# Attention with split-precision matmuls: values products of 512 columns, half of the long ones turned into x's place

## The reference

```python
# x: [1024, 512]; 32 query heads, 8 key/value heads, 32 latent heads, head size 128
q  = rope(x @ w_q);  k = rope(x @ w_k);  v = x @ w_v
lq = x @ w_lq;       lk = rope(lq @ w_lk);  lv = x @ w_lv
attn = causal_attn(q, repeat(k, 4), repeat(v, 4))     # softmax(q k^T / sqrt(128)) v
lat  = causal_attn(q, lk, lv)
x = layernorm(x + attn @ w_o + lat @ w_lo)
# top-1 routed low-rank FFN
logits = x @ route_w.T;  route_weight = one_hot(argmax) * max
out = ((route_weight[..., None] * (x @ A)) @ Bw)
x = layernorm(x + out)
```

## Time and profile before

| what | value |
|---|---|
| median of 3 runs | 2001.11 us (2000.52 to 2001.81) |
| the profiled execution | 2000.62 us |
| its span, first to last instruction | 1998.5 us |
| PE busy | 1974.5 us (99%), 12640 matmuls |
| DVE, POOL, ACT busy | 1352.9, 1127.4, 1064.4 us |
| mean granted TensorE clock | 0.999 |

### The profile page before, as it was taken

The page is one execution under the profiler, slowest core; times in us unless marked ns, Lnnn a source line. Parts: engine busy times, 40 slices in busy tenths (PEclk is TensorE's granted clock), DMA queues, the critical chain, the costliest instruction groups (busy, mean ns, idle before and its releaser), DMA issues.

```text
span 1998.5 us, 33651 instructions
## 1 busy us (share of the span) xinstructions
PE 1974.5 (99%) x12640; PEld 1804.9 (90%) x12640; DVE 1352.9 (68%) x3370; ACT 1064.4 (53%) x2463; POOL 1127.4 (56%) x904
## 2 busy tenths in 40 slices
PE   8999999999999999999999999999999999999997
PEld 7989989899898989989899898998989989898995
DVE  7758668585675757757577684766757577575766
ACT  3736628365372744727357373563726547274564
POOL 6637566375664647646475564656646565564750
PEclk9999999999999999999999999999999999999999
DMA  5010010101000010000100001000010100100001
GB/s 179 12 35 1 22 35 12 35 1 44 12 22 25 1 56 1 22 25 1 56 1 22 24 5 52 1 22 25 22 35 1 42 5 22 35 12 22 1 12 43
DMA packets 19296, 50.14 MB, mean 25 GB/s; under 512 B 5824, under 2 KB 7872, under 8 KB 19008
## 3 DMA queue, kind: packets, MB, share of 16 engines
q1 hardware_dynamic: 18992, 45.90, 6.9%
q10 hardware_dynamic: 144, 2.10, 0.2%
HBM read 45.89 MB, written 2.10 MB: 24 GB/s over the span
## 4 chain that ended last, share of the span: by engine, by line
PE 88%; POOL 5%; DVE 4%; ACT 2%; issue 1%; DMA 0%; ACTq 0%; SPq 0%; DVEq 0%
PE ps L388 25%; PE ps L390 25%; PE ps L389 25%; PE ps L474 13%; POOL probs L827 3%; POOL ql_lo L831 2%; DVE probs L883 1%; DVE probs L882 1%; DVE probs L884 1%; ACT probs L660 1%; DVE val_lo L848 0%; DVE probs L908 0%; ACT ql_hi L631 0%; ACT acc L727 0%; PE ps L587 0%
## 5 line engine op out<-in xcount | busy, mean ns | idle before, releaser
L836 POOL TENSOR_TENSOR probs<-probs,inv_sum 128x640 f32<-128x640 f32 (+7 forms) x512 | 583.4, 1151 | 343.7 <-DVE inv_sum L915 342.7
L908 DVE CUSTOM_DVE_ANT_0 probs<-ps,mask 128x640 f32<-128x640 f32 (+7 forms) x512 | 384.6, 754 | 167.1 <-PE ps L390 120.3
L848 DVE TENSOR_TENSOR pt_lo<-ps,pt_hi 128x512 fp32r<-128x512 f32 (+3 forms) x768 | 399.2, 548 | 74.9 <-ACT pt_hi L631 73.1
L631 ACT ACTIVATE pt_hi<-ps 128x512 fp32r<-128x512 f32 (+3 forms) x768 | 347.0, 487 | 163.6 <-PE ps L474 160.3
L660 ACT ACTIVATE probs<-probs,neg_max 128x640 f32<-128x640 f32 (+7 forms) x512 | 396.9, 775 | 61.0 <-DVE neg_max L908 49.9
L388 PE MATMUL ps<-pt_hi,val_hi 128*128 128x256 f32 x1216 | 353.8, 291 | 0.0
L389 PE MATMUL ps<-pt_lo,val_hi 128*128 128x256 f32 x1216 | 342.6, 282 | 0.0
L390 PE MATMUL ps<-pt_hi,val_lo 128*128 128x256 f32 x1216 | 342.3, 282 | 0.0
L474 PE MATMUL ps<-ident,probs 128*128 128x128 f32 x2304 | 335.0, 273 | 0.0
L827 POOL TENSOR_TENSOR probs<-probs 128x512 f32<-128x512 f32 x144 | 186.5, 1295 | 210.7 <-DVE probs L884 210.7
L631 ACT ACTIVATE ql_hi<-probs 128x512 fp32r<-128x512 f32 x128 | 80.9, 632 | 415.3 <-POOL probs L827 415.3
(11 more groups left out here) (101 smaller groups left out, 4099.6 us busy)
## 6 DMA issues: line engine op xcount, KB each, us to landing
raw<-wo SPq DMA_DIRECT2D x32, 512.0 KB, 3.3
raw<-wq SPq DMA_DIRECT2D x16, 512.0 KB, 3.2
raw<-wlv SPq DMA_DIRECT2D x16, 512.0 KB, 3.7
raw<-wkv SPq DMA_DIRECT2D x8, 512.0 KB, 3.4
acc<-xT SPq DMA_DIRECT2D x4, 512.0 KB, 5.5
wlk_raw<-wlk SPq DMA_DIRECT2D x16, 128.0 KB, 3.1
acc<-x ACTq DMA_DIRECT2D x1, 2048.0 KB, 10.3
out<-acc SPq DMA_DIRECT2D x8, 256.0 KB, 2.0
```

Of the source, the lines that this page charges most:

```text
L631: return nc.scalar.activation(dst, src, ACT.Copy)
L836: nc.gpsimd.tensor_tensor(b, b, inv_sum[:, k % 8:k % 8 + 1].to_broadcast([P, b.shape[-1]]), ALU.mult).then_inc(q["normed"], 1)
L848: return nc.vector.tensor_tensor(dst, src, h, ALU.subtract)
L908: nc.vector.tensor_tensor_reduce(out=probs_of(n).rearrange("p (b n) -> p b n", b=b), in0=scores_of(n), in1=mask[:, S - w:S].rearrange("p ( ...
```

## The change

- Values products cover four query tiles, 512 columns, and there are 8 per pair (`CHUNKS = TILES // 4`). Even products take the short tiles of a latent head or of the plain heads, odd ones the long tiles. Block j of a product starts at the first column that needs it (`first_column`). `PV_BEFORE` and `PV_AFTER` place them: slots 13, 16, 21, 24, 29, 31, 36, 36.
- Odd products hold 8 blocks x 512 columns of turned probabilities. Products 3 and 7 have them in parts 0 and 1 of `pt_hi`, `pt_lo`; products 1 and 5 in `x_hi`, `x_lo` (`turned_probs`). x is therefore stored once in device memory (`x_kept`) and read back in every pair but the last (`bring_x_back`: four DMAs on ACT's queue behind the high part of product 5). PE waits for it (`x_back`) ahead of the two units of query head 0.
- The order of units changes; three `v` units instead of one are put off into the attention slots.
- The first two units of pair 1 (both `lk`) are made in the outputs stage of pair 0 (`AHEAD`).
- The order of output steps and tiles, the slots of output weights and the slots of the high and low parts of products (`O_SLOT`) change; `HI_LAG` is 2; one output is added in slot 37.

```diff
@@
-CHUNKS = TILES // 2
+STEP_ORDER = ((1, 0), (0, 0), (1, 1), (0, 1))
+CHUNKS = TILES // 4
-O_BANKS = (6, 7)
+O_BANKS = (7, 6, 6, 7)
+LATE_BANKS = (6, 7)
-OUT_HI_SLOT = (16, 24)
-OUT_LO_TILE = (17, 25)
+OUT_HI_SLOT = (20, 27)
+OUT_LO_TILE = (19, 31)
-    [("q", 0, 0), ("q", 0, 1), ("lk", 0, 0), ("v", 0), ("lk", 0, 1), ("v", 1), ("q", 1, 0), ("q", 1, 1), ("lk", 1, 0), ("v", 2), ("lk", 1, 1), ("v", 3), ("k", 0, 0), ("k", 0, 1), ("v", 4), ("v", 5), ("v", 6), ("v", 7)],
-    [("q", 0, 0), ("lk", 0, 0), ("q", 0, 1), ("v", 0), ("lk", 0, 1), ("q", 1, 0), ("v", 1), ("lk", 1, 0), ("q", 1, 1), ("v", 2), ("lk", 1, 1), ("v", 3), ("v", 4), ("v", 5), ("v", 6), ("v", 7)],
+    [("q", 0, 0), ("q", 0, 1), ("lk", 0, 0), ("v", 0), ("lk", 0, 1), ("q", 1, 0), ("v", 4), ("lk", 1, 0), ("q", 1, 1), ("v", 1), ("lk", 1, 1), ("k", 0, 0), ("k", 0, 1), ("v", 5), ("v", 2), ("v", 6), ("v", 3), ("v", 7)],
+    [("lk", 0, 0), ("lk", 0, 1), ("q", 0, 0), ("lk", 1, 0), ("q", 0, 1), ("v", 0), ("lk", 1, 1), ("q", 1, 0), ("v", 4), ("q", 1, 1), ("v", 1), ("v", 5), ("v", 2), ("v", 6), ("v", 3), ("v", 7)],
-LATE = ({6: 17}, {6: 15})
+LATE = ({4: 15, 7: 16, 10: 17}, {3: 13, 7: 14, 9: 15})
-OUT_ORDER = tuple(i for pair in HEADS_AT_ONCE for i in pair)
-HEAD = {34: ((0, 0, 2),), 35: ((1, 0, 2), (2, 0, 2)), 36: ((0, 2, 4), (1, 2, 4))}
+OUT_ORDER = (3, 2, 4, 5, 1, 0, 6, 7)
+HEAD = {32: ((0, 0, 2),), 34: ((1, 0, 2),), 35: ((2, 0, 2), (0, 2, 4)), 36: ((1, 2, 4),)}
+def tiles_of(m):
+    return range(m // 2 * 8 + 1 - m % 2, m // 2 * 8 + 8, 2)
+def column_of(n):
+    a, latent, i = tile_of(n)
+    return P * (i % 4) if latent else 256 * (i % 2) + P * a
+def first_column(m, j):
+    return min(column_of(n) for n in tiles_of(m) if tile_of(n)[2] >= j)
+PV_BEFORE = {13: ((0, 0, 4),), 21: ((2, 0, 4),), 29: ((4, 0, 4),), 36: ((6, 0, 2),)}
+PV_AFTER = {16: ((1, 0, 8),), 24: ((3, 0, 8),), 31: ((5, 0, 6),), 36: ((7, 0, 8),)}
+O_SLOT = {16: (0,), 19: (1,), 22: (2,), 27: (3,), 29: (4,), 34: (5,), 36: (6,), 38: (7,)}
+AHEAD = ({}, {5: (0,), 6: (1,)})
+ADD_SLOT = {37: (0,)}
-HI_LAG = 3
+HI_LAG = 2
@@ def block_kernel
+        kept = nc.dram_tensor("x_kept", [2, 2, P, CT * 512], F32, kind="Internal").ap()
+        def turned_probs(m):
+            if m % 2 == 0:
+                return [w[:, 2, :].rearrange("p (j n) -> p j n", n=512) for w in (pt_hi, pt_lo)]
+            if m % 4 == 1:
+                return [w[:].rearrange("p c (h n) -> p (c h) n", h=2) for w in (x_hi, x_lo)]
+            return [w[:, 0:2].rearrange("p a (j n) -> p (a j) n", n=512) for w in (pt_hi, pt_lo)]
+        def x_half(h):
+            return [w[:, :, 512 * h:512 * h + 512].bitcast(F32) for w in (x_hi, x_lo)]
@@ unit
+                    if kind == "q" and x == 0 and (g, pair) != (0, 0):
+                        pe.wait_ge(x_back[h], 32 * (g * PAIRS + pair))
@@ with_values
                 for j in range(j0, j1):
-                    q0 = P if latent and j == last else 0
-                    at = 256 * (first + j)
-                    mm = three(ps[:, O_BANKS[m % len(O_BANKS)], 256 * (m % 2) + q0:256 * (m % 2) + 256], [w[:, j, :] for w in vals],
-                               [w[:, half, at + q0:at + 256] for w in (pt_hi, pt_lo)], j == 0, j == last)
+                    q0 = first_column(m, j)
+                    mm = three(ps[:, bank, q0:512], [w[:, j, :] for w in vals], [w[:, j, q0:512] for w in turned_probs(m)],
+                               j == 0, j == last)
@@ scalar
+            def bring_x_back():
+                for h in range(2):
+                    for part, dst in enumerate(x_half(h)):
+                        nc.scalar.dma_start(dst, kept[h, part].rearrange("p (c n) -> p c n", c=CT)).then_inc(x_back[h], 16)
@@ scalar, start
             nc.scalar.dma_start(acc[:], x).then_inc(q["res_in"], 16)
+            for h in range(2):
+                for part, src in enumerate(x_half(h)):
+                    nc.scalar.dma_start(kept[h, part].rearrange("p (c n) -> p c n", c=CT), src).then_inc(q["x_saved"], 16)
@@ scalar, slots
-                        if k in O_SLOT:
-                            output_hi(g, pair, O_SLOT[k])
+                        for m in O_SLOT.get(k, ()):
+                            output_hi(g, pair, m)
+                            if m == 5 and (g, pair) != (GROUPS - 1, PAIRS - 1):
+                                bring_x_back()
```

More of the change, by code:

```diff
@@ L145, in bank_of, with values_until @@
 def bank_of(pair, u):
-    return 4 + u % BANKS if u < regular(pair) else O_BANKS[u - regular(pair)]
+    return 4 + u % BANKS if u < regular(pair) else LATE_BANKS[(u - regular(pair)) % 2]
+def values_until(pair, u):
+    return sum(x[0] == "v" for x in UNITS[pair][:u + 1])
 def unit_in_bank(pair, u):
@@ L241, in block_kernel @@
         raw_in = [sem(f"raw_in{i}") for i in range(RAW_SLOTS)]
+        x_back = [sem(f"x_back{h}") for h in range(2)]
         def per_pair(g, pair, n, k):
@@ L476, in turn_probs, with with_values @@
                     mm.then_inc(q["turned"], 1)
[L478 to L482, removed]
+            def with_values(g, pair, m, j0, j1):
+                a, latent, _ = tile_of(max(tiles_of(m)))
+                last = blocks_of_product(m) - 1
+                bank = O_BANKS[m % len(O_BANKS)]
                 if j0 == 0:
-                    pe.wait_ge(q["pt_lo_made"], per_pair(g, pair, T_UNITS, UNITS_BEFORE[n + 1]))
-                    if m == 0:
+                    pe.wait_ge(q["pt_lo_made"], per_pair(g, pair, T_UNITS, UNITS_BEFORE[max(tiles_of(m)) + 1]))
+                    if m < 2:
                         pe.wait_ge(q["val_lo_made"], per_pair(g, pair, ST, ST))
                         pe.wait_ge(q["rope_mul"], rope_base(g, pair, ROPES[pair]))
-                    if m >= len(O_BANKS):
-                        pe.wait_ge(q["o_lo_made"], per_pair(g, pair, CHUNKS, m - len(O_BANKS) + 1))
+                    else:
+                        user = max(x for x in range(m) if O_BANKS[x % len(O_BANKS)] == bank)
+                        pe.wait_ge(q["o_lo_made"], per_pair(g, pair, CHUNKS, user + 1))
                 vals = [w[:, 1 + a if latent else 0] for w in (val_hi, val_lo)]
                 for j in range(j0, j1):
-                    q0 = P if latent and j == last else 0
-                    at = 256 * (first + j)
-                    mm = three(ps[:, O_BANKS[m % len(O_BANKS)], 256 * (m % 2) + q0:256 * (m % 2) + 256], [w[:, j, :] for w in vals],
-                               [w[:, half, at + q0:at + 256] for w in (pt_hi, pt_lo)], j == 0, j == last)
+                    q0 = first_column(m, j)
+                    mm = three(ps[:, bank, q0:512], [w[:, j, :] for w in vals], [w[:, j, q0:512] for w in turned_probs(m)],
+                               j == 0, j == last)
                 if j1 == last + 1:
@@ L508, in outputs @@
                 for step in range(step0, step1):
[L509 to L513, removed]
+                    latent, a = STEP_ORDER[step]
+                    if y == 0 and latent:
+                        pe.wait_ge(q["wo_lo"], SEED + per_pair(g, pair, len(OUT_PARTS), a + 1))
+                        pe.wait_ge(q["o_lo_made"], per_pair(g, pair, CHUNKS, 2 * (a + 1)))
+                    if (latent, a) == (0, 0):
+                        pe.wait_ge(q["o_lo_made"], per_pair(g, pair, CHUNKS, chunk_with(t) + 1))
                     out, weights = output_step(step)
@@ L523, in _ @@
                 for pair in range(PAIRS):
-                    for u in range(regular(pair)):
+                    for u in range(units_ahead(g, pair), regular(pair)):
                         if u == regular(pair) - EARLY_UNIT:
@@ L553, in _ @@
                             outputs(g, pair, y, BEGUN.get(y, 0), STEPS)
+                        for u in begun_behind(g, pair, y):
+                            unit(*next_pair(g, pair), u)
             ra = raw[:, 0, 0:CT * (E + E * R)].rearrange("p (c n) -> p c n", c=CT)
@@ L647, in probs_hi @@
             def probs_hi(g, pair, n):
-                half, first, q0 = part_of_pt(n)
-                dst = pt_hi[:, half, :].rearrange("p (j n) -> p j n", j=ST)
+                q0, dst = column_of(n), turned_probs(chunk_of(n))[0]
+                if (g, pair, n) == (0, 0, 0):
+                    act.wait_ge(q["x_saved"], 64)
                 for x, (b0, b1) in enumerate(blocks_of(n)):
@@ L669, in rope_hi @@
             def rope_hi(g, pair, r):
+                u = ROPE_UNITS[pair][r]
+                if u < units_ahead(g, pair) and UNITS[pair][u][2] == 1:
+                    act.wait_ge(q["out_mm"], SEED + per_pair(g, pair, ST, 0))
                 act.wait_ge(q["rope_add"], rope_base(g, pair, r + 1))
@@ L893, in probs_lo @@
             def probs_lo(g, pair, n):
-                half, first, q0 = part_of_pt(n)
-                h, l = (w[:, half, :].rearrange("p (j n) -> p j n", j=ST) for w in (pt_hi, pt_lo))
+                q0, (h, l) = column_of(n), turned_probs(chunk_of(n))
                 for x, (b0, b1) in enumerate(blocks_of(n)):
```

(14 more changed lines are left out.)

89 lines of the change are left out of this document (43 added, 46 removed).

## The result

The changed kernel takes 2020.99 us (median of 4 runs, 2019.74 to 2022.30) against 2001.46 beside it: ratio 1.0096, 95% interval 1.0078 to 1.0113. It is 1.0% slower where I had forecast 1.4% faster. Both the time and the direction are wrong.

The account below looks back on a forecast made before the run. The prediction took PE to bound the kernel. From 2000.6 us it took 24 (width) and 12 (changes of kind) and added 6 (waits) and 2 (start): 1972.6, rounded to 1973 us, 1.4% faster, range 1959 to 1995.

Parts of the forecast that it names:

- (a): Attention slots without a values product: PE waits for DVE between nothing and 4.8 us a pair; 0.4 taken, 6 us.
- (b): POOL subtracts output weights before scaling tile 20 for slot 24: hidden; if not, about 1 us a pair.
- (c): Reading x back from slot 34 on ACT's queue: landing hidden behind PE's work, issue holding 1.5 us, at no cost.
- fewer changes of kind: Attention slots: fewer values products behind transposes, more scores behind them; saves 0.74 us a pair, 12 us in all.
- (d): Kernel start: four more DMA issues on ACT ahead of its first weights cost 2 us, once.
- What a matmul costs, fewer and wider values matmuls: Values products: from distances between starts, 512-column matmuls save 1.5 us a pair, 24 us in 16 pairs.
- The 4 us worked out from an isolated gap: Values products: saving by the Trainium skill's page, N/2.4 + 2.5 ns per matmul; set aside for the trace's 24 us.
- the slack of two tiles: Slots without a product: scores may run two tiles (2.5 us) ahead, set against DVE falling 1.6 us behind.
- DVE paces the bare slots: Rival: the 21 slots without a product run at 1.67 us instead of 1.25, 56 us more, 2023; chance 0.07.
- ACT held: Rival: in slot 34 DMA issues hold ACT or x lands late, 4.5 us in 15 pairs, 68 us, 2041; chance 0.06.
- (e): Start of pair 1: the two units made ahead only start DVE and POOL earlier; nothing gained.

Follow-up runs that it names:

- e8: e1 with long values products 1, 3 and 5 cut by blocks over neighbouring slots, same matmuls; 1978.09 us, ratio 0.9884.
- e3: The changed kernel with each values matmul wider than 256 columns split in two at column 256; 2042.86 us, 21.9 more than the change.
- e5: e1 with POOL subtracting its first part of the output weights behind tile 21 instead of tile 19; 2001.43 us, 7.4 less than e1.
- e1: The changed kernel with the first store of x issued on SP's queue instead of ACT's; 2008.87 us, ratio 1.0034.
- e7: e1 with no units made ahead of pair 1; 2013.37 us, 4.5 more than e1.
- e2: The changed kernel without the return of x, its four DMAs per pair and PE's waits left out; 2018.76 us, ratio 1.0083.

## Why the prediction was wrong

Two terms of the sum failed. The first is (a), *bare slots*, and with it (b) and (c): I put 6 us, 0.4 a pair, for waits, and the runs show 35, about 2.3 a pair (1.9 that e8 recovers, POOL's wait among them, and 0.6 in each pair 1 in slot 34). The second is *fewer changes of kind*: I put 12 us, and there is nothing to be saved. A smaller miss is (d), 9 us at the start instead of 2.

- *What a matmul costs, fewer and wider values matmuls (24 us)*: right. Distances of 0.229 against 0.226 us, and 21.9 us in e3. The 4 us worked out from an isolated gap would have been far too little. The values matmuls take 1.9 us a pair less, of which 1.5 is the width; the late first distance behind transposes moved from them to the scores.
- *Fewer changes of kind (12 us)*: wrong. I took 0.09 us for a transpose from three of them, which include the short last distance. At 0.109 seven take 0.76, and the 0.69 measured are less, not more. So the price of 0.14 us for a start behind transposes, and that of 0.08 for scores, left out what the last transpose gives back, and the number of runs of transposes didn't change.
- *(a) bare slots (6 us)*: 31 us (e8). My own sum for slots 17 to 20 was good, PE 5.0 and DVE 6.6 us where DVE shows 6.4. The step that failed is the choice near the lower bound, with the slack of two tiles as the reason and slots 3 to 7 as the model. Those have a values unit in the middle, and DVE makes its first `pt_lo` only in slot 5. The rival "DVE paces the bare slots" was right on the mechanism in slots 17 to 20 and 26 to 28, and put 56 us. At slot 16 it isn't DVE's work but the way from scores over the maximum to the scores two tiles on: a wide tile is followed by a narrow one and nothing else.
- *(b) POOL behind tile 19*: named, called hidden, "if not, about 1 us a pair". It was 0.5 (e5). I had reckoned "over 6 us later"; at 704.3 ACT made the high part, POOL subtracted from 705.4 to 707.8, and PE was ready for the scaled tile some 0.5 us before it came.
- *(c) x comes back*: right on the landing. No q unit waits for it, and the DMA share of the outputs stretch rose (0.50 where it was 0.36 in the kernel before, for a pair 1). The rival "ACT held" exists in a small form: 4.3 to 4.9 us of holding in a pair 1 instead of 1.5, and 0.6 us lost. In a pair 0, with 3.0 us of holding, nothing is lost.
- *(d) the start (2 us)*: mechanism right, size wrong: 8.8 us, of which 2.3 are the lower clock behind the wait. I took 0.37 us for each issue from the one DMA of long runs, where the earlier trace rows also show a DMA of short runs that held its engine for 5.3 us; and ACT at the start has no cover. With the stores on SP's queue (e1) the start costs 1.3 us, near the 2.
- *(e) two units ahead*: I said nothing is gained; e7 shows 4.5 us.

The sum with what was measured: 2000.6 - 24 (width) - 0 (kinds) + 31 (bunched products) + 4 (slot 34) + 9 (start) = 2020.6, and 2021.0 was measured. With both causes removed, e8 runs at 1978.1. That is 2000.6 - 24 + 1.4 (its start), so the width is all that is gained, and its nearness to the forecast of 1973 is partly luck: 12 us of changes of kind that aren't there stand against 6 us of waits that spreading removes.

## What to carry to other kernels

Fusing work of the bottleneck engine into fewer and longer pieces saves its fixed costs, and takes away the filling beside which other engines did their work; weigh each place between a producer and its consumer two steps on, and each run of slots without filling, not the average of the stretch. Where a long piece is a sum over blocks, keep the wide matmuls and spread the blocks: the width and the cover can both be had (1978 us against 2021 and 2001). Count a change of kind on both sides before its saving goes into a sum: what follows was late by as much as the last transpose was short. And the issue of a big DMA can hold its engine for microseconds; put the first big stores on an engine with nothing due.

## What the runs showed of the hardware

- Four DMAs of 1024 KB in 2 KB runs, issued one behind the other on ACT's queue behind a 2048 KB load, held ACT for 0.61, 0.96, 4.30 and 3.55 us; the loads of the same size in slot 34 took 0.53, 0.65, about 0.9 and 0.5 to 3.0 us. No PE row waits for their landing (9.8 and 11.7 us median for parts of x).
- 63 MB read back over the run cost nothing measurable in e1: its pairs are as long as e2's, to 0.05 us.
- The busy time of PE did not tell of the change: 1972.5 against 1974.5 us for 1536 matmuls less. Distances between starts did.
- The granted clock was 1.00 up to the wait at the start of the changed kernel, 0.50 when PE resumed behind 4.15 us of standing, and 1.00 again from about 35 us on. In e1 and in the kernel before, where PE stands for less than 1 us at a time there, it is 1.00 from 10 to 50 us.
- Transposes of 128x128 f32 start 0.109 us apart; the last is followed after 0.028 us, and the next start is 0.08 us later than is even, whether scores or values follow.
